# Causal masks from diagonal 64 by 64 products and staircase rows, pads set once outside Pool, and projections and expert products at other steps

## The reference

```python
# layers 0 and 1 (convolutions): non-local block with batch norm, then quantised 1x1, 3x3 depthwise,
# 3x3 and 1x1 convolutions; they are outside the change
# layers 2 and 3, attention (stages 0 and 2), for each of 8 images, 16 heads of 16 channels, 256 tokens:
h = layernorm(x)
q, k, v = split(h @ w_in + b_in)
s = q @ k.T * 16 ** -0.5          # layer 2 adds slope[h] * (key - query)
s = where(key <= query, s, -inf)   # causal
x = x + softmax(s) @ v @ w_out + b_out
# layer 2, second half (stage 1): x = x + layernorm(x) @ ternary(weight).T
# layer 3, second half (stage 3): a router picks 2 of 8 experts for each token
g = top-2 softmax of (layernorm(x) @ Wr.T + br)
x = x + sum_e g[e] * (layernorm(x) @ We[e] + be[e]) @ Wo + bo
```

## Time and profile before

| | |
|---|---|
| median of 3 runs | 728.45 us (727.65 to 730.27) |
| the profiled execution | 728.74 us, its span 727.0 us |
| granted TensorE clock, mean | 0.944 |
| busy of the span: TensorE, its weight loads, VectorE, ScalarE, Pool | 88%, 54%, 65%, 44%, 20% |
| DMA queue 1, share of 16 engines over the span | 48.1% |
| chain that ended last | TensorE 63%, VectorE 10%, ScalarE 4%, DMA 2% |

### The profile page before, as it was taken

The page is one execution under the profiler, slowest core; times in us unless marked ns, Lnnn a source line. Parts: engine busy times, 40 slices in busy tenths (PEclk is TensorE's granted clock), DMA queues, the critical chain, the costliest instruction groups (busy, mean ns, idle before and its releaser), DMA issues.

```text
span 727.0 us, 11229 instructions
## 1 busy us (share of the span) xinstructions
PE 637.3 (88%) x4204; PEld 393.0 (54%) x4204; DVE 476.1 (65%) x1267; ACT 319.0 (44%) x547; POOL 143.4 (20%) x126
## 2 busy tenths in 40 slices
PE   6887666367699999999999999999999999999987
PEld 3754224244366666666666665555565564545443
DVE  4777566756857766766766767675747666665544
ACT  2476465023355555565556554343343434343110
POOL 2230001455532332331232131102020200000000
PEclk9889985687889999999999999999999999999989
DMA  9300001787928958957946955907337190000000
GB/s 345 158 0 1 0 0 18 98 110 75 119 59 78 117 82 73 120 84 66 131 80 73 112 87 64 112 17 98 33 81 65 37 109 16 1 15 1 15 15 14
DMA packets 83229, 50.51 MB, mean 69 GB/s; under 512 B 4036, under 2 KB 82628, under 8 KB 82884
## 3 DMA queue, kind: packets, MB, share of 16 engines
q1 hardware_dynamic: 83176, 49.81, 48.1%
HBM read 35.11 MB, written 14.68 MB: 68 GB/s over the span
## 4 chain that ended last, share of the span: by engine, by line
PE 63%; DVE 10%; ACT 4%; DMA 2%; issue 2%; SPq 1%; DVEq 0%; POOL 0%; ACTq 0%
PE ps L1242 14%; PE ps L1128 10%; PE ps L1119 7%; PE ps L1188 5%; PE ps L1199 4%; PE ps L1184 4%; PE ps L1111 3%; PE ps L1167 3%; PE ps L1213 3%; PE ps L1206 2%; DVE nparts L1390 2%; DVE acc L1459 2%; PE ps L1162 2%; DVE nmax L1381 2%; DMA KS<-parts_dram 2%
## 5 line engine op out<-in xcount | busy, mean ns | idle before, releaser
L1381 DVE TENSOR_REDUCE nmax<-ps 128x2 f32<-128x512 f32 (+1 forms) x192 | 130.5, 687 | 86.7 <-PE ps L1167 47.4
L1285 ACT ACTIVATE PT<-ps 128x512 f32<-128x512 f32 x192 | 114.8, 599 | 126.4 <-PE ps L1188 124.7
L1242 PE MATMUL ps<-wm,xnT 128*128 128x512 f32 x256 | 122.8, 610 | 0.0
L1055 POOL TENSOR_TENSOR rstd<-ve,fix 128x2 f32<-128x2 f32 x32 | 22.2, 693 | 337.8 <-DVE ve L1343 337.8
L1279 ACT ACTIVATE QS<-ps 8x1024 bf16<-8x1024 f32 x64 | 65.0, 1016 | 51.2 <-PE ps L1172 50.5
L1188 PE MATMUL ps<-QS,KS 110*128 110x256 bf16 (+3 forms) x512 | 74.7, 248 | 0.0
L1459 DVE SCALAR_TENSOR_TENSOR acc<-ps,gate,acc 128x256 f32<-128x256 f32 x128 | 61.6, 481 | 19.9 <-PE ps L1242 17.5
L1091 POOL TENSOR_TENSOR parts<-rest,fix 128x512 bf16<-128x512 f32 x30 | 38.0, 1268 | 159.5 <-DVE rest L1361 105.7
L1242 PEld LDWEIGHTS ps<-wm,xnT 128*128 128x128 f32 x256 | 46.1, 193 | 40.7 <-issue 40.1
L1119 PE MATMUL ps<-xnT,wt 128*128 128x256 f32 x256 | 65.2, 402 | 1.4 <-ACT xnT L1258 1.4
L1184 PE MATMUL ps<-fixb 128*128 128x256 bf16 (+1 forms) x192 | 60.6, 316 | 0.9 <-ACT QS L1279 0.3
(11 more groups left out here) (205 smaller groups left out, 1006.0 us busy)
## 6 DMA issues: line engine op xcount, KB each, us to landing
parts_dram<-parts SPq DMA_DIRECT2D x32, 384.0 KB, 3.1
QS<-parts_dram SPq DMA_DIRECT2D x96, 128.0 KB
KS<-parts_dram SPq DMA_DIRECT2D x96, 128.0 KB, 9.5
wt<-wt_dram SPq DMA_DIRECT2D x1, 2562.0 KB, 18.6
wm<-wm_dram SPq DMA_DIRECT2D x1, 2449.0 KB, 13.0
xc<-x_dram SPq DMA_DIRECT2D x8, 256.0 KB, 5.2
out_dram<-res SPq DMA_DIRECT2D x8, 256.0 KB, 2.1
w<-w_dram SPq DMA_DIRECT2D x1, 845.0 KB, 7.6
```

The source lines that it names most:

```text
L1242: mm = pe.matmul(d, normT(stage, batch)[:, c, t * P:(t + 1) * P], M("We", c * EXPERTS * CH + e * 2 * CH, 2 * CH), start=(c == 0), stop=(c ...
L1285: act.activation(PT[:, n % PT_RING, :], bank(piece), ACT.Exp).then_inc(drain(piece), 1)
L1381: dve.tensor_reduce(group[:, 0, :] if part == 0 else group[:, 1, 2 * part - 2:2 * part], bank(piece).rearrange("p (j n) -> p j n", n=w_), ...
```

## The change

- **Masks.** The mask product at the start of each unit is gone. At the end of each unit stand two products of 64 rows, 64 output columns (partitions) and, for each head, 64 moving columns: one on array rows and columns 0 to 63, one on 64 to 127 (L1177 in S, L1200 in X). They mask the two diagonal 64 by 64 blocks of the unit.
- **Staircase rows.** What lies above the diagonal outside these blocks is masked by 3 new rows of the stacks, between the 8 maximum rows and the bias rows. Row k of `QS` is 1 for the k-th 64 queries, row k of `KS` is -1e30 for keys from the next 64 on. Every product of S and X now has 107 rows, or 113 in stage 0. So S reads the 8 maximum rows in stage 2 too, and the zero fill of `QS` is issued for bodies 3 to 15 instead of 0 to 7.
- **Pads.** PAD is one piece, of the first body. VectorE sets V's constants for all three buffers and computes small tables; ScalarE writes 11 rows of `QS` and of `KS` of buffer 0, 4096 elements each (L1293, L1297); SyncE waits for that and copies them to buffers 1 and 2 with four DMAs (L1060).
- **Steps.** V goes from -10 to -14, LOAD from -11, -10 to -12, -11. The projection pieces of body 1 stand 6 steps earlier and those of body 2 twelve (`AHEAD`). E goes from 33..41 to 35..42 and CT from 43 to 44; `gate` has two buffers for this.

The diff, cut:

```diff
+HALF = P // 2
+STEPS = PIX // HALF
+STEP_AT = MAX_AT + MAX_ROWS
+BIAS_AT = STEP_AT + STEPS - 1
...
-        ("SPLIT", 0, 0, -15), ("K", 0, 0, -15), ("SPLIT", 0, 1, -14), ("LOAD", 0, 0, -11), ("LOAD", 0, 1, -10),
-        ("V", 0, 0, -10), ("PAD", 0, 0, -9), ("AT", 0, 0, 22), ("PR", 0, 0, 23), ("LNa", 1, 0, 24), ("LNb", 1, 0, 25),
+        ("SPLIT", 0, 0, -15), ("K", 0, 0, -15), ("SPLIT", 0, 1, -14), ("V", 0, 0, -14), ("LOAD", 0, 0, -12),
+        ("LOAD", 0, 1, -11), ("AT", 0, 0, 22), ("PR", 0, 0, 23), ("LNa", 1, 0, 24), ("LNb", 1, 0, 25),
...
-        ("GB", 3, 0, 32), ("E", 3, 0, 33), ("E", 3, 1, 34), ("E", 3, 2, 35), ("E", 3, 3, 36), ("E", 3, 4, 37),
-        ("E", 3, 5, 39), ("E", 3, 6, 40), ("E", 3, 7, 41), ("CT", 3, 0, 43)),
+        ("GB", 3, 0, 32), ("E", 3, 0, 35), ("E", 3, 1, 36), ("E", 3, 2, 37), ("E", 3, 3, 38), ("E", 3, 4, 39),
+        ("E", 3, 5, 40), ("E", 3, 6, 41), ("E", 3, 7, 42), ("CT", 3, 0, 44)),
...
+AHEAD = {1: 6, 2: 12}
...
+            if step < 0:
+                step -= AHEAD.get(at, 0)
...
-                    if stage == 0 and n == 0:
+                    if n == 0 and body(stage, batch) >= STACKS:
                         zeros = fixb_in[P - 1:P, FIXB["tri0"][0]:FIXB["tri0"][0] + 4 * P].bitcast(BF16)
...
+                if kind == "PAD":
+                    wait(sp, "chosen", piece)
+                    for k in range(1, STACKS):
+                        for stacks in (QS, KS):
+                            sp.dma_start(stacks[MAX_AT:BIAS_AT, k], stacks[MAX_AT:BIAS_AT, 0])\
+                                .then_inc(sems["chosen_spread"], 16)
...
-                    pool.tensor_tensor(KS[MAX_AT:MAX_AT + MAX_ROWS, stack(stage, batch)]
-                                       .rearrange("p (g h) n -> p g h n", h=half), *one_per_row, ALU.add)\
-                        .then_inc(sems["padded"], 1)
...
-                    r = rows_of(0) if stage == 0 else slice(0, STACK)
+                    r = rows_of(stage)
                     if part == 0:
-                        pe.matmul(d, FB("ident"), FB("tri0"), start=True, stop=False, skip_group_check=True)
...
+                    heads = 4 if part == 0 else 2
+                    for x in range(2):
+                        block = slice(x * HALF, (x + 1) * HALF)
+                        triangles = FB("tri0", 0, heads * P).rearrange("p (j n) -> p j n", n=P)
+                        mm = pe.matmul(diagonal[block, :, block], FB("ident")[block, block], triangles[block, :, block],
+                                       start=False, stop=True, skip_group_check=True)
...
-                    pe.matmul(d.rearrange("p (j n) -> p j n", n=width)[:, :, 0:P], FB("tri0", 0, P),
-                              FB("ident").unsqueeze(1).broadcast_to([P, len(heads), P]), start=True, stop=False,
-                              skip_group_check=True)
...
+                    for x in range(2):
+                        block = slice(x * HALF, (x + 1) * HALF)
+                        mm = pe.matmul(diagonal[block, :, block], FB("tri0", 0, P)[block, block],
+                                       FB("ident")[block, block].unsqueeze(1).broadcast_to([HALF, len(heads), HALF]),
+                                       start=False, stop=True, skip_group_check=True)
...
+                if kind == "PAD":
+                    rows = slice(MAX_AT, BIAS_AT)
+                    spread = [BIAS_AT - MAX_AT, HEADS, STEPS, HALF]
+                    act.wait_ge(fixb_loaded, 16)
+                    act.activation(QS[rows, 0].rearrange("p h (k n) -> p h k n", k=STEPS),
+                                   FB("ident", STEP_AT, STEPS)[rows, :].unsqueeze(1).unsqueeze(3).broadcast_to(spread),
+                                   ACT.Copy).then_inc(sems["chosen"], 1)
+                    wait(act, "dve_step", piece)
+                    act.activation(KS[rows, 0].rearrange("p h (k n) -> p h k n", k=STEPS),
+                                   chosen[rows].unsqueeze(3).broadcast_to(spread), ACT.Copy).then_inc(sems["chosen"], 1)
...
+                if kind == "PAD":
+                    pads = V[:].rearrange("p a t h s -> p (a t h) s")
+                    dve.memset(pads[:, :, DH + 1:], 0.0).then_inc(sems["padded"], 1)
...
+                    wait(dve, "gates_ready", ("RT", stage, batch, 3))
```

More of the change, by code:

```diff
@@ L141, in in_order @@
             out.append(((BODY * at + step, group, 0, -at, k), (kind, s, b, n)))
-        for k, (kind, stage, n, step) in enumerate(FLOW[s]):
+        for k, (kind, stage, n, step) in enumerate(FLOW[s] + ((("PAD", 0, 0, -13),) if at == 0 else ())):
+            if step < 0:
+                step -= AHEAD.get(at, 0)
             place = (step, 1) if engines == "tensor" else (step + 1, 1) if kind in LONG else (step, 2)
@@ L1445, in vector_piece @@
                     settle(dve.tensor_tensor(one, one, E, ALU.mult))
-                    dve.tensor_tensor(gate[:], one, wide(m), ALU.mult).then_inc(sems["gates_ready"], 1)
+                    dve.tensor_tensor(gate[:, par], one, wide(m), ALU.mult).then_inc(sems["gates_ready"], 1)
                 if kind == "GB":
```

71 lines of the change are left out of this document (39 added, 32 removed), and 2 rows, old and new, of the table FLOW.

## The result

| | before | after |
|---|---|---|
| median (range) | 728.7 us (727.65 to 730.27) | 756.8 us (755.21 to 757.38) |
| ratio, 95% interval | | 1.038 (1.0355 to 1.0406) |
| span of the profiled execution | 727.0 | 754.6 |
| mean granted clock | 0.944 | 0.932 |
| TensorE busy | 88% | 91% |

The changed kernel is 28.1 us slower, and the forecast was 736. The first lines of the page of after: busy time and share of each engine, then the granted clock in 40 slices of 18.9 us, then the engines' shares of the chain that ended last.

What follows compares the result with a forecast made beforehand. The prediction took TensorE to bound the kernel from 215 us on, and loads and VectorE before. Its sum was 728.7 + 26 (masks) - 10 (start) - 6 (gates) - 3 (AT and PR) = 735.7, say 736; range 710 to 749, its own 727 to 747.

Steps and rivals of the forecast that it cites:

- the bound: TensorE bounds the kernel from 215 to 680 us, with only about 12 us idle there.
- rival 1: Shape changes around the mask pairs (L1177, L1200) are cheap: faster below 0.079 us each, 686 us at zero; chance 0.22.
- Rival 2: The two mask products of a pair, writing to one PSUM bank, don't overlap: 25 us not saved, 759 us; chance 0.10.
- the price of a pair: Masks in S and X: 576 added shape changes at 0.092 us cost 53, columns save 25; +26 us with 15/16 counted.
- the start: Bodies 0 to 3: no Pool stop but later loads, S of body 3 at 232 us; -10 us (0 to -15).
- the gates: GT's 6.3 us of waits for VectorE's gates, covered by moving E 7 behind them: -6 us (0 to -8).
- AT and PR: PR's 5.1 us wait for ScalarE's copy of `attnT` shrinks with V ahead of AT: -3 us (0 to -5).

Runs made afterwards that it cites:

- a_oldmask: The changed kernel with the whole-array mask product put back ahead of each unit's products, all else as changed; 714.6 us, ratio 0.981 to the kernel before.
- g_first2: The changed kernel with whole-array masks in bodies 0 and 1 alone, the 64 by 64 pairs kept in bodies 2 to 15; 741.3 us.
- i_oldmask_oldE: The changed kernel with whole-array masks and with E and CT back at their old steps (E 33 to 41, CT 43); 717.0 us.
- b_noahead: The changed kernel, pairs kept, with the projections of bodies 1 and 2 back at their own steps (AHEAD empty); 748.1 us.
- f_twice: The changed kernel with every pair of 64 by 64 mask products issued twice, one pair right behind the other; 772.4 us.
- d: The changed kernel with whole-array masks and without the projections of bodies 1 and 2 moved ahead; 715.9 us.
- c: The changed kernel, pairs kept, with all steps as before the change: no projections ahead, V, LOAD, E and CT at old steps; 757.4 us.

## Why the prediction was wrong, step by step

**Right: the bound, and the sign.** TensorE bounds the steady bodies, and the masks lose. Nothing supports rival 1: the change of shape costs 0.09 in and 0.12 out, and a body takes 28.3 us, not under 26.4. Rival 2's time, 759, is close to what was measured, but its cause is refuted: the products of a pair overlap (28.2 us a body with one, 28.3 with both), and its sign, a body of 29.6, did not come. The Trainium skill, TensorEngine Tiling (Array Packing), Gotcha 1: PSUM Pressure, says that different row tiles cannot access one PSUM bank at the same time. For these two parts of the array, which write to separate partitions of one bank, the runs say otherwise, with 0.17 us to the next start for one product as for two. The sign given for rival 1, a body under 26.4, was too strict by the prediction's own sum: at the break-even price of 0.079, 36 changes a body make 26.8 - 1.6 - 0.4 + 2.8 = 27.6. The measured 28.3 is above both.

**Mis-sized: the price of a pair.** Forecast 1.7 us a body, measured 2.05 in stage 0 and 1.8 in stage 3 (26.0 us against 32 for 16 bodies without the clock's part). The number of changes was right. The way out was taken from rows where M is left, 0.09, and is 0.12 for a pair. Six ways in at 0.095, three out at 0.12 and three times 0.03 more ahead of M, O0 or O1 make 4.1 us a body; less some 1.9 for the columns saved, this gives 2.2. Two things were in no term. Three float32 projections a body stand right behind a pair, and their first pass takes 0.32 us to the next start, against 0.27 to 0.29 behind X's full-array products: 0.13 more, 2.4 in all. And part of it falls into time that was idle: in a steady body a_oldmask has two waits which after has not, of 0.22 us behind M and of 0.17 ahead of PR, by the distances of starts. The first of them in the timeline of a_oldmask, where X's mask begins 0.42 us behind M, while after has 0.21 there (403.52 to 403.73):

```profile
396.44 0.28 PE L1178 MATMUL ps<-fixb,nparts 128*8 128x128 bf16 x2
396.86 0.28 PE L1190 MATMUL ps<-fixb 128*128 128x256 bf16 x1
```

So a body's pairs cost 2.4 us, of which 2.05 are seen.

**Failed: the start.** The step was "Body 2's begins after 34.4 less the stop (6.9) and less some 2.5 of cold clock, at 205, and body 3's at 232", together with a price of the masks (+26 us, 15/16 of 16 bodies) that is the same wherever they stand. The first half was right as a statement on the constants and loads: with whole-array masks the starts are 164.2, 182.0, 206.2 and 232.5, and S of body 3 comes 9.6 us earlier than before (forecast 10). The second half failed. The change moves the projections of bodies 1 and 2 out of this stretch and replaces full-array mask products there by small ones, and among what is left, scores and pairs above all, the granted clock comes back late after the stall: 37.6 us at half clock instead of 6.8. That is 9 to 10 us on top of the masks' own cost, by the difference at the start (15.4 less three bodies at 2.05) and by g_first2 (14.5 less 4). The prediction added its terms as if they were independent. Rows that should have raised the question were there: a cold clock was part of the 34.4 us, and it was not asked what in this stretch had ended it.

**Too large: the gates.** Forecast -6, measured -2.4 in the medians. The waits went as forecast (6.3 to 1.0 us). What the term left out are the waits that the same pieces of E had covered where they stood: PR's of the last three bodies and AT's of the last, 2.7 us, which are there in a_oldmask and not in i_oldmask_oldE. A moved cover was costed where it arrives, not where it leaves.

**Right: AT and PR.** With whole-array masks a steady body of stage 0 is 26.3 instead of 26.7 (the mean of seven); over the 7 bodies from 3 to 9 that is some 3 us, the term's -3. The wait went from 5.1 us to none in i_oldmask_oldE; the 1.6 that a_oldmask has are those behind the later E.

The terms as measured: masks in steady form 32 to 33, the clock at the start 9 to 10, the start itself -9.6, bodies 3 to 9 -2.9, and from S of body 10 to the end -2.0. That is 42.2 - 14.5 = 27.7; the spans differ by 27.6.

Two sums of the prediction are off. S of body 3 "near 234 (232 and two bodies' masks)" should be 235, at 1.7 us for each of two bodies. And the upper end of the forecast's own range, 747, lets only the start fail; with the start, the gates and AT and PR all at nothing the recorded terms give 728.7 + 26 = 754.7. Even that is under the 756.8 measured, since no term had the clock in it.

What stays open: why the clock comes back so late among scores and pairs. The runs show only that it hangs on what TensorE executes in that stretch: it is back after 6.8 us among whole-array masks without any projection (a_oldmask), at 180.3 with pairs and projections (b_noahead), at 183.3 with each pair twice and no projection (f_twice). In a_oldmask the masks stand ahead of each unit's products again as well as being whole, so place and shape were not tried apart; the changes counted from starts explain the price without the place. The last body of i_oldmask_oldE, where E stands as before, is still 1.6 us longer than before; it has 3.4 us more at half clock (667.4 to 670.8), and what brings that is not shown. That the gain at the start is Pool's constant rows is by exclusion (not AHEAD, by d; not the steps, by c against b); no run put them back alone.

## What to carry to other kernels

Price a small product on part of the array by its two changes of shape (here 0.09 in, 0.12 out) before its columns; a pair of 128 columns in place of a product of 256 saved 0.06 us and paid 0.2, and only several such products behind one change can pay. When work is moved, ask what it did where it stood, as a cover for a wait or as work among which the clock came back, and not only what it does where it goes. Of a bundle of edits, run the parts alone: here one part cost 42 us and hid a gain of 14.
